# A four-layer graph network on one core: the first group graph by graph, the last two groups in one body, and products whose two halves take turns

## The reference

```python
def L0(x, adj):        # h = x W + b, then adj h, divided by the row sums of adj
    return einsum(adj, x @ W + b) / adj.sum(-1)
def L1(x, adj):        # relu((adj x) K), masked where a row of x is all zero
    return relu((adj @ x) @ K) * mask(x)
def L2(x, adj):        # normalised adjacency: dh = rsqrt(rowsum(adj + I))
    return relu((dh * (adj + I) * dh) @ x @ K2 + bias)
def L3(x, adj):        # attention and two diffusion steps
    e = leaky_relu(sj[None, :] + si[:, None] + ab)    # sj, si: (x Wv + bv) times two vectors
    T = normalise_rows(adj * exp(e))
    return relu(x Wk[0] + T x Wk[1] + T T x Wk[2] + sum of bk)
for L in (L0, L1, L2, L3):
    x = layernorm(x + L(x, adj))
```

## Time and profile before

| | us |
|---|---|
| median of 3 runs | 566.76 |
| the runs | 564.90, 566.76, 567.08 |
| the profiled execution, as timed | 566.34 |
| its span, first to last instruction | 564.5 |
| TensorE busy | 534.0 (95%) |
| VectorE busy | 502.2 (89%) |
| GpSimd busy | 459.8 (81%) |
| ScalarE busy | 418.0 (74%) |
| mean granted clock of TensorE, share of full speed | 0.992 |

### The profile page before, as it was taken

The page is one execution under the profiler, slowest core; times in us unless marked ns, Lnnn a source line. Parts: engine busy times, 40 slices in busy tenths (PEclk is TensorE's granted clock), DMA queues, the critical chain, the costliest instruction groups (busy, mean ns, idle before and its releaser), DMA issues.

```text
span 564.5 us, 12239 instructions
## 1 busy us (share of the span) xinstructions
PE 534.0 (95%) x4044; PEld 511.2 (91%) x4044; DVE 502.2 (89%) x1221; ACT 418.0 (74%) x929; POOL 459.8 (81%) x575
## 2 busy tenths in 40 slices
PE   5698999999999999999999999999999999988973
PEld 5698999999999999999999999999899999988863
DVE  3888989989999889989899899998899898998686
ACT  5468787687976878687886879768886968765653
POOL 3968898989988899988989799888989888753243
PEclk9999999999999999999999999999999999999997
DMA  8724011350042301522123401323104200202001
GB/s 278 272 63 140 24 39 58 113 167 19 19 130 74 130 19 37 149 98 69 37 62 106 167 19 32 117 77 127 36 20 149 94 1 1 76 2 75 0 1 74
DMA packets 25222, 44.73 MB, mean 79 GB/s; under 512 B 3184, under 2 KB 3824, under 8 KB 25200
## 3 DMA queue, kind: packets, MB, share of 16 engines
q1 hardware_dynamic: 24336, 43.79, 24.1%
q10 hardware_dynamic: 864, 0.66, 0.4%
HBM read 36.05 MB, written 8.39 MB: 79 GB/s over the span
## 4 chain that ended last, share of the span: by engine, by line
PE 84%; DVE 10%; ACT 2%; issue 2%; POOL 1%; DMA 1%; ACTq 0%; DVEq 0%; POOLq 0%
PE pair L261 15%; PE pair L263 15%; PE pair L262 15%; PE ring L261 12%; PE ring L263 12%; PE ring L262 12%; PE ring L331 2%; DVE stats L1194 2%; PE ring L355 1%; DVE ring L1274 1%; DVE fea_lo L1186 1%; DVE alpha_lo L1210 1%; DMA P<-w_dram 1%; DVE P L1266 1%; DVE X L1279 1%
## 5 line engine op out<-in xcount | busy, mean ns | idle before, releaser
L629 ACT ACTIVATE X<-X,nmr,rstd 128x256 f32<-128x256 f32 x192 | 103.2, 592 | 48.9 <-POOL nmr L931 48.9
L914 POOL TENSOR_TENSOR rstd<-powin,minus_half 128x2 f32<-128x2 f32 (+1 forms) x124 | 103.3, 836 | 39.4 <-DVE nmean L1200 39.2
L1194 DVE BATCH_NORM_STATS2 stats<-X 128x6 f32<-128x512 f32 x128 | 89.6, 705 | 1.2
L261 PE MATMUL ring<-adj_hi,nod_lo 128*128 128x256 f32 x256 | 73.9, 289 | 5.5 <-DVE nod_lo L1232 3.1
L548 ACT ACTIVATE fea_hi<-ring 128x512 fp32r<-128x512 f32 x96 | 56.8, 593 | 25.1 <-PE ring L263 19.4
L262 PE MATMUL ring<-adj_lo,nod_hi 128*128 128x256 f32 x256 | 73.0, 285 | 0.0
L263 PE MATMUL ring<-adj_hi,nod_hi 128*128 128x256 f32 x256 | 73.0, 285 | 0.0
L261 PE MATMUL ring<-W_hi,fea_lo 128*128 128x256 f32 x256 | 72.5, 283 | 0.5 <-DVE fea_lo L1186 0.4
L263 PE MATMUL ring<-W_hi,fea_hi 128*128 128x256 f32 x256 | 71.7, 280 | 0.0
L262 PE MATMUL ring<-W_lo,fea_hi 128*128 128x256 f32 x256 | 71.3, 279 | 0.0
L1186 DVE TENSOR_TENSOR fea_lo<-ring,fea_hi 128x512 fp32r<-128x512 f32 x96 | 63.7, 682 | 7.7 <-ACT fea_hi L548 7.3
(11 more groups left out here) (113 smaller groups left out, 2042.9 us busy)
## 6 DMA issues: line engine op xcount, KB each, us to landing
adj_in<-adjT_dram SPq DMA_DIRECT2D x64, 256.0 KB, 2.8
xT_in<-xT_dram SPq DMA_DIRECT2D x32, 256.0 KB, 3.7
X<-x_dram SPq DMA_DIRECT2D x32, 256.0 KB, 2.6
out_dram<-X SPq DMA_DIRECT2D x32, 256.0 KB, 2.0
P<-wk_dram SPq DMA_DIRECT2D x3, 256.0 KB, 4.0
P<-w_dram SPq DMA_DIRECT2D x2, 256.0 KB, 5.8
X<-bk_dram SPq DMA_DIRECT2D x3, 128.0 KB, 4.1
P<-w_dram ACTq DMA_DIRECT2D x1, 256.0 KB, 3.9
```

The lines of the kernel that those rows point to most:

```text
L261: mm(o, lhs(1, t, i), rhs(0, t), start=t == 0, stop=False)
L629: last = nc.scalar.activation(nodes(X[min(l + 1, 3)][g])[:, t, :], nodes(X[l][g])[:, t, :], ACT.Identity, scale=rstd[l][g][:, t:t + 1], bi ...
L914: tt(rstd[l][g][:, 0:n], powin[l][g][:, 0:n], minus_half[:, 0:n], ALU.pow).then_inc(rstd_ready[l], 1)
L1194: nc.vector.bn_stats(stats[l][g][:, :], by_turns(X[l][g])).then_inc(st_ready[l], 1)
```

## The change

1. **First group, graph by graph.** SP loads xT, adj and x of graph 0, then of graph 1, and so on. ACT and DVE take the splits in that order too, and s1, s2 of graph 0 come ahead of s1 of graphs 1 to 3. s1 of group 0 writes to the ring banks (`h_bank(g, first=True)`), and s2(g) waits for its own h only. `attention_vectors` (line 375, twelve small matmuls) moves behind s3(1, 0), to a bank of `pair1`, with a wait for y0 of graph 3; the wait of s3(0, 0) for its result goes, and s1 of graphs 2 and 3 of group 1 get it. On POOL `first_degree_power` moves behind `norm0`. On DVE `w1_lo`, `attention_constants` and `weights_lo` move to later places.
2. **Idle transposes.** `warm_up`: PE starts with 20 transposes of the identity into a bank of `pair0`, whose result nobody reads.
3. **Halves by turns.** `product_by_turns` does the same twelve matmuls as `product`, but half 0 and half 1 alternate. s2, s8a, s8b and s10 use it in every group.
4. **Last two passes in one body.** `last_iterations` takes the place of `late_iteration` and `last_iteration`. It holds the same steps of groups 6 and 7, mixed: s6 and s7 of the last group begin ahead of s11(3) and s5(3) of the body, and in the last products s11(0) comes ahead of s10(3).
5. The loop's order (`iteration`) is unchanged.

The diff, cut to its core (the order tables are shown by their rows below):

```diff
@@ sync
-            for load in (load_xT, load_adj, load_x):
-                for g in range(SLOTS):
+            for g in range(SLOTS):
+                for load in (load_xT, load_adj, load_x):
                     load(g, 0, before=False)
@@
-        def h_bank(g):
-            return pair[g // 2][:, g % 2, :]
+        def h_bank(g, first=False):
+            return ring[g][:, :] if first else pair[g // 2][:, g % 2, :]
@@ tensor
+            def product_by_turns(dst, lhs, rhs):
+                for t in range(2):
+                    for left, right in ((1, 0), (0, 1), (0, 0)):
+                        for i, o in enumerate(dst):
+                            last = mm(o, lhs(left, t, i), rhs(right, t), start=t == 0 and left == 1,
+                                      stop=t == 1 and left == right)
+                return last
@@ s1
                 elif kn == 1:
                     pe.wait_ge(y_ready[0][2 + g // 2], 1)
+                    if g >= 2:
+                        pe.wait_ge(e_const_ready, 2)
@@ s2
-                pe.wait_ge(h_ready, count(min(2 * g + 1, 3), kn))
+                pe.wait_ge(h_ready, count(g if first else min(2 * g + 1, 3), kn))
@@ s2, s8a, s8b, s10
-                product([pair[g % 2][:, i, 0:FA] for i in range(2)], cols(adj, g),
+                product_by_turns([pair[g % 2][:, i, 0:FA] for i in range(2)], cols(adj, g),
@@ s3
-                if first and g == 0:
-                    pe.wait_ge(e_const_ready, 2)
@@
+            def warm_up():
+                pe.wait_ge(pool_c, 2)
+                for i in range(WARM_UP):
+                    nc.tensor.transpose(pair[0][:, 0, 0:P], ident[:, :], ident[:, :])
@@ attention_vectors
                 pe.wait_ge(aw_loaded, AW_LOADED)
+                pe.wait_ge(y_ready[0][3], 1)
@@ tensor, first_iteration
+                s1(0, 0, first=True)
                 s2(0, 0, first=True)
-                attention_vectors()
+                s1(1, 0, first=True)
+                s1(2, 0, first=True)
+                s1(3, 0, first=True)
                 s2(1, 0, first=True)
                 s2(2, 0, first=True)
                 s2(3, 0, first=True)
+                s1(0, 1, first=True)
                 s3(0, 0, first=True)
-                s1(0, 1, first=True)
-                s1(1, 1, first=True)
-                s1(2, 1, first=True)
                 s3(1, 0, first=True)
+                attention_vectors()
@@ tensor, last_iterations, the place where the two groups meet (all lines new)
+                s11(1, k)
+                s3(3, k + 1)
+                s11(2, k)
+                s5(0, k + 1)
+                s4(3, k + 1)
+                s6(0, k + 1)
+                s5(1, k + 1)
+                s5(2, k + 1)
+                s11(3, k)
+                s6(1, k + 1)
+                s6(2, k + 1)
+                s7(0, k + 1)
+                s5(3, k + 1)
+                s8a(0, k + 1, last=True)
@@ tensor, last_iterations, its end
+                s10(2, k + 1)
+                s11(0, k + 1, last=True)
+                s10(3, k + 1)
+                s11(1, k + 1, last=True)
+                s11(2, k + 1, last=True)
+                s11(3, k + 1, last=True)
```

More of the change, by code:

```diff
@@ L28 @@
 EPS = 1e-5
+WARM_UP = 20
 FP = mybir.dt.float32
@@ L286, in s1 @@
                     pe.wait_ge(y_ready[0][2 + g // 2], 1)
-                product([h_bank(g)[:, 0:N], h_bank(g)[:, N:2 * N]], cols((xT_hi, xT_lo), g),
-                        lambda s, t: W0[s][:, t, :]).then_inc(s1_done, 1)
+                    if g >= 2:
+                        pe.wait_ge(e_const_ready, 2)
+                bank = h_bank(g, first and kn == 0)
+                product([bank[:, 0:N], bank[:, N:2 * N]], cols((xT_hi, xT_lo), g), lambda s, t: W0[s][:, t, :]).then_inc(s1_done, 1)
             def s2(g, kn, first=False):
-                pe.wait_ge(h_ready, count(min(2 * g + 1, 3), kn))
+                pe.wait_ge(h_ready, count(g if first else min(2 * g + 1, 3), kn))
                 pe.wait_ge(adj_ready, count(g, kn))
@@ L340, in s8a @@
                     pe.wait_ge(z0_ready, count(2, k))
-                product([pair[0][:, i, 0:FA] for i in range(2)], cols(fea, g),
+                product_by_turns([pair[0][:, i, 0:FA] for i in range(2)], cols(fea, g),
                         lambda s, t: WA[s][:, t, :]).then_inc(s8a_done, 1)
@@ L348, in s8b @@
                     pe.wait_ge(z0_ready, count(3, k))
-                product([pair[1][:, i, :] for i in range(2)], cols(fea, g),
+                product_by_turns([pair[1][:, i, :] for i in range(2)], cols(fea, g),
                         lambda s, t: WB[s][:, t, :]).then_inc(s8b_done, 1)
@@ L365, in s10 @@
                     pe.wait_ge(Q_ready, count(g - 2, k))
-                product([pair[g % 2][:, i, 0:FA] for i in range(2)], cols(alpha, g),
+                product_by_turns([pair[g % 2][:, i, 0:FA] for i in range(2)], cols(alpha, g),
                         lambda s, t: mixed((h_hi, h_lo)[s][g])[:, t, :]).then_inc(s10_done, 1)
@@ new lines, in last_iterations @@
+                s8a(0, k + 1, last=True)
+                s8b(0, k + 1, last=True)
+                s7(1, k + 1)
+                s9(0, k + 1)
+                s6(3, k + 1)
+                s8a(1, k + 1, last=True)
+                s7(2, k + 1)
+                s8b(1, k + 1, last=True)
+                s8a(2, k + 1, last=True)
+                s9(1, k + 1)
+                s7(3, k + 1)
+                s8b(2, k + 1, last=True)
+                s9(2, k + 1)
+                s8a(3, k + 1, last=True)
@@ L535, in _ @@
+                s8b(3, k + 1, last=True)
+                s9(3, k + 1)
+                s10(0, k + 1)
+                s10(1, k + 1)
+                s10(2, k + 1)
[4 more added lines that the diff above has]
+                s11(3, k + 1, last=True)
+            warm_up()
             pe.wait_ge(w0_ready, 1)
-            for g in range(SLOTS):
-                s1(g, 0, first=True)
             first_iteration()
@@ L548, in copy, with h_hi_part @@
                 return nc.scalar.activation(dst, src, ACT.Copy)
-            def h_hi_part(g, kn):
+            def h_hi_part(g, kn, first=False):
                 act.wait_ge(s1_done, count(g, kn))
-                copy(mixed(h_hi[g])[:, :, 0:F], nodes(h_bank(g))).then_inc(h_hi_ready, 1)
+                copy(mixed(h_hi[g])[:, :, 0:F], nodes(h_bank(g, first))).then_inc(h_hi_ready, 1)
             def z0(g, kn):
@@ L874, in _ @@
+                p12(3, k + 1)
+                alpha_hi_part(2, k + 1)
+                logits(3, k + 1)
+                exp(3, k + 1)
+                q_hi(0, k + 1)
+                alpha_hi_part(3, k + 1)
+                q_hi(1, k + 1)
+                q_hi(2, k + 1)
+                q_hi(3, k + 1)
+                norm(3, 0, k + 1)
+                norm(3, 1, k + 1)
+                norm(3, 2, k + 1)
+                norm(3, 3, k + 1)
             act.dma_start(W0_in, w0.rearrange("p (t f) -> p t f", t=2)).then_inc(w0_loaded, 16)
@@ L882, in _ @@
             copy(W0[0][:, :, :], W0_in).then_inc(w0_hi_ready, 1)
-            for g in range(SLOTS):
-                xT_hi_part(g, 0)
             first_iteration()
@@ new lines, in last_iterations @@
+                y2(2, k + 1)
+                p0(0, k + 1)
+                y2b(2, k + 1)
+                from_ring(3, t2_hi_ready, k + 1, t2_ready)
+                statistics(2, 2, k + 1)
+                variance_eps(2, 2, k + 1)
+                from_ring(1, x3T_hi_ready, k + 1, x3T_ready)
+                variance_eps(3, 3, k)
+                y2(3, k + 1)
+                p2_lo(0, k + 1)
+                y2b(3, k + 1)
+                statistics(2, 3, k + 1)
+                p0(1, k + 1)
@@ new lines, in last_iterations @@
+                leaky(0, k + 1)
+                variance_eps(2, 3, k + 1)
+                from_ring(2, x3T_hi_ready, k + 1, x3T_ready)
+                p2_lo(1, k + 1)
+                from_ring(3, x3T_hi_ready, k + 1, x3T_ready)
+                leaky(1, k + 1)
+                p0(2, k + 1)
+                p2_lo(2, k + 1)
+                p0(3, k + 1)
+                leaky(2, k + 1)
+                alpha_lo_part(0, k + 1)
+                p2_lo(3, k + 1)
+                alpha_lo_part(1, k + 1)
@@ L1679, in _ @@
             tt(W0[1][:, :, :], W0_in, W0[0][:, :, :], ALU.subtract).then_inc(w0_ready, 1)
-            for g in range(SLOTS):
-                dve.wait_ge(xT_hi_ready, g + 1)
-                tt(xT_lo[g][:, :], xT_in[g][:, :], xT_hi[g][:, :], ALU.subtract).then_inc(first_xT_ready, 1)
             first_iteration()
```

673 lines of the change are left out of this document (304 added, 369 removed).

## The result

| | before | changed | predicted |
|---|---|---|---|
| median, us | 566.92 (564.9 to 568.9, 4 runs) | 560.57 (560.3 to 562.4, 4 runs) | 561.3 |
| ratio to before, 95% interval | 1 | 0.988 [0.9852, 0.9908] | 0.990 |
| profiled execution, as timed / span | 566.34 / 564.5 | 560.77 / 559.0 | |

The account below looks back on a forecast made before the run. TensorE, busy 95% and never stopping in the loop, was taken as the bound, with gaps outside it. -0.3 - 1.3 + 0.8 - 3.5 - 1.1 = -5.4 us from 566.3 gave 560.9, median 561.3; range 558 to 564.5, with rivals 555 to 567.5.

Parts of the forecast that it names:

- Up to y0(0): Start of the kernel to the first y0, 20.84 us before: -0.3 us, ending near 20.5.
- The load chain: First group: xT of graph 3, now the tenth load, lands at 13.4; its copy, splits and s1(3) follow until 17.6.
- the slack of 2.3 us: First group: TensorE has this slack before s1(3), so no saving was booked for the idle transposes.
- The rival with steps of 0.21 us in s1(3): First group: clock still low at s1(3), y0(0) 1.1 us later, +0.8 instead of -0.3; chance a quarter.
- To the loop: First y0 to the loop, 32.60 us before: -1.3 us, with VectorE bounding at 31.3 us.
- By turns: Products with alternating halves: 0.6 ns more on each of 1408 steps, +0.8 us, range -2.8 to +4.2.
- Rival A: Products by turns: every change of bank costs 8 ns, 11.3 us instead of 0.8, giving 571.8 us; chance 0.1.
- Late passes: Last two passes up to s10 of the last group, 94.92 us before: one body fills TensorE's holes, -3.5 us.
- The term of 3.0 us for five named waits: Late passes: VectorE, late behind `p2_lo(3, k)`, makes s6(0), s5(2), s5(3), s8a(2) and s8b(3) wait, 3.0 us in all.
- Tail: From s10 of the last group to the end, 23.04 us before: -1.1 us, s11(0) filling the hole before s10(3).
- B: VectorE eats it: gains before the loop and in the late passes shrink to -1 together, 565.1 us; chance 0.18.
- C: All holes close: -3.3 before the loop, late passes at 88.0 (-6.9), giving 555.9 us; chance 0.12.

Follow-up runs that it names:

- e1: The changed kernel without its 20 idle transposes; ratio to before 0.9894.
- e5: The changed kernel with x + b, y0 and statistics of graph 0 moved earlier in the first group; 558.74 us, ratio to before 0.9857.
- e7: The changed kernel with the last group's steps from s10(0) on in the order of the kernel before; ratio to before 0.9889.
- e9: e5 with sums and y0 of graph 1 moved ahead of x1_lo(0) on VectorE; ratio to before 0.984.
- e3: The kernel before with only the last two passes joined in one body; ratio to before 0.9894.
- e10: The changed kernel with one ScalarE norm of group 7 moved earlier, so that its store is issued sooner; 559.27 us, ratio to before 0.985.
- e11: e9 and e10 together, plus the splits of the weights moved behind graph 2's operand of s5; ratio to before 0.9932.

## Why the prediction was right, point by point

The time came out 0.7 us under the forecast, and the pieces add up to -5.5 us against -5.4. That is better than the terms deserve, and it is luck: they missed by +0.3, +0.4, -1.2, +0.7 and -0.3 us, which cancel.

- **Up to y0(0): -0.3 predicted, 0.0.** The load chain is what sets it, as said, and h_lo(3) ended at 17.76 (17.6 predicted). The step that failed is the two x + b: 2.37 us instead of 1.4, since one xT_lo on GpSimd was enough to stretch the first. That TensorE had the slack of 2.3 us was wrong: before s1(3) it had 0.3 us, so the transposes are worth up to 1.2 us here. The rival with steps of 0.21 us in s1(3) didn't occur; in e1 the delay came with s1(3) at 0.12, because the products ahead of it were late. The 0.0 is one pair of executions, within what the loads move (e1 above). And the premise that h of graph 3 must come ahead of y0(0) was an order, not a dependence: e5 ended y0(0) at 14.06.
- **To the loop: -1.3 predicted, -0.86.** VectorE bounds, as said, with 29.97 us (30.6 predicted); its waits were 1.8 us instead of 0.7. s3(0, 0) came 6.6 us behind y0(0) (6.5 predicted).
- **By turns: +0.8 predicted, -0.4 in the loop.** Its range held it. 0.6 ns more a step was read from rows good to 10 ns; it was 0.5 ns less: a pass took 65.44 us, 65.52 before. Rival A had no ground.
- **Late passes: -3.5 predicted, -2.84, and -4.6 at best.** The mechanism was right: one body fills the holes. The term of 3.0 us for five named waits was too dear: 0.47 us for s6(0) (0.8 predicted), 0.45 for s5(2) (1.0), 0.23 for s8b(3) (0.3), under 0.2 for s8a(2) (0.4). So idle time didn't merely move to s5 and s6 of the last group. The stall of 3 us behind `p2_lo(3, k)` isn't in the trace; VectorE's longest there is 1.65 us at 476.86, behind alpha_hi, and its longest of all in these passes 1.97 at 536.53, ahead of s10. And the step left out two things: the norm of the last group overwrites what group 6 still stores, 1.2 us in both profiles of the changed kernel and none in six of its variants, and a power on GpSimd was stretched, 0.5 us.
- **Tail: -1.1 predicted, -1.36.** z3(3) began 14.28 us behind s10(0), 15.68 before. By e7 the order gave only 0.45; the other 0.95 goes with alpha_lo(3) not being stretched, which the earlier trace rows showed and the step didn't book.
- **The clock.** It is 1.00 in the late passes (0.98 before), and 0.95 behind y0(0), where it cost nothing. s1(0) stepped by 0.12 us behind the transposes and by 0.21 without. The Trainium skill (TensorE: Matmul & The Clock Gate, Part 4 (PE-mode transpose)) says that transposes don't count as activity for the clock gate. This trace disagrees, and the measurement decides; in one execution (e9, last section) the level stayed low behind the transposes all the same.
- **Rivals.** B and C were the right places: C's late passes (88.0) were half reached by e3 and e10 (90.3), B's VectorE bounds the first group.

## What to carry to other kernels

Where a kernel has no slack in its loop, look at its ends: joining the last two passes was worth up to 4.6 us and the tail 1.4 (0.45 of it by the new order), and a hand-written order hid 2 us more in the first group, because an operation that was ready stood behind one that waited. When two passes are joined, list every buffer that the second writes and the first still stores, and issue those stores first; and move a block of work only after reading what stands behind its new place on every queue, since e11 turned a wait of 0.9 us into one of 4.8.
